# Four transformer blocks on one core: GpSimd takes the ends of 24 splits, SyncE takes the small transfers of the maxima, and the work is put in another order

## The reference

```python
    xn = _adaln(x, noise_emb, ln1_w, ln1_b)
    q, k, v = jnp.split(xn @ qkv_w.T, 3, axis=-1)
    q = _rope(q.reshape(B, L, N_HEADS, HEAD_DIM))
    k = _rope(k.reshape(B, L, N_HEADS, HEAD_DIM))
    sa = _attn(q, k, v) @ sa_out_w.T
    x = res + sa
    ...
    q = _rope((xn @ q_w.T).reshape(B, L, N_HEADS, HEAD_DIM))
    k = _rope((context @ k_w.T).reshape(B, L_ctx, N_HEADS, HEAD_DIM))
    v = (context @ v_w.T).reshape(B, L_ctx, N_HEADS, HEAD_DIM)
    x = res + _attn(q, k, v) @ ca_out_w.T
    ...
    h = jax.nn.gelu(xn @ ffn_w1.T + ffn_b1, approximate=False)
    x = res + (h @ ffn_w2.T + ffn_b2)
```

## Time and profile before

| | us |
|---|---|
| median of 3 runs | 2908.04 |
| lowest and highest | 2906.6, 2916.17 |
| the profiled execution | 2916.84 |
| its span | 2915.0 |

### The profile page before, as it was taken

The page is one execution under the profiler, slowest core; times in us unless marked ns, Lnnn a source line. Parts: engine busy times, 40 slices in busy tenths (PEclk is TensorE's granted clock), DMA queues, the critical chain, the costliest instruction groups (busy, mean ns, idle before and its releaser), DMA issues. The chain is left out here.

```text
span 2915.0 us, 47676 instructions
## 1 busy us (share of the span) xinstructions
PE 2728.5 (94%) x15136; PEld 1351.8 (46%) x15136; DVE 1893.7 (65%) x4209; ACT 1425.8 (49%) x2579; POOL 590.3 (20%) x999
## 2 busy tenths in 40 slices
PE   8999999999989999999988888898999999999899
PEld 5444344335544424334455566656645323224456
DVE  5977388642574783866344889668974884885621
ACT  3455635574445583566644444333221674785441
POOL 2110001131331110331125323411020010112510
PEclk9999999999999999999998999999999999999899
DMA  6333122433452312233066516521420322123621
GB/s 207 69 104 107 41 72 71 112 89 98 144 172 53 114 51 67 91 115 95 22 186 186 167 50 195 146 85 60 147 60 1 116 60 52 45 61 108 183 92 38
DMA packets 268153, 286.78 MB, mean 98 GB/s; under 512 B 70665, under 2 KB 207243, under 8 KB 267275
## 3 DMA queue, kind: packets, MB, share of 16 engines
q1 hardware_dynamic: 256651, 282.28, 33.0%
q0 software_dynamic: 11264, 1.46, 0.3%
HBM read 167.43 MB, written 114.72 MB: 97 GB/s over the span
## 5 line engine op out<-in xcount | busy, mean ns | idle before, releaser
L1570 ACT ACTIVATE probs<-ring_b 128x512 f32<-128x512 f32 (+1 forms) x1728 | 921.8, 599 | 457.9 <-PE ring_b L1429 359.9
L1748 DVE TENSOR_REDUCE row_max<-ring_a 128x1 f32<-128x1024 f32 x512 | 602.0, 1218 | 151.7 <-PE ring_a L1385 150.9
L1429 PE MATMUL ring_b<-q_ring,k_ring 100*128 100x512 bf16 x1536 | 526.8, 381 | 10.5 <-ACT probs L1570 2.8
L1385 PE MATMUL ring_a<-k_ring,q_ring 96*128 96x512 bf16 x1536 | 450.1, 383 | 27.9 <-DVE row_max L1748 16.1
L1462 PE MATMUL ring_c<-probs,v_and_ones 128*17 128x512 f32 x3072 | 402.0, 599 | 1.8 <-ACT probs L1570 1.2
L1745 DVE CUSTOM_DVE_ANT_0 w_mlp<-ring_a,w_mlp 128x1024 bf16<-128x1024 f32 x256 | 302.1, 1222 | 49.6 <-PE ring_a L1385 48.4
L1868 POOL CAST neg_max_parts<-neg_max 16x128 bf16<-16x128 f32 x112 | 37.6, 336 | 1392.1 <-ACT neg_max L1564 1141.3
L1429 PEld LDWEIGHTS ring_b<-q_ring,k_ring 100*128 100x128 bf16 x1536 | 145.7, 97 | 349.9 <-issue 241.5
L1385 PEld LDWEIGHTS ring_a<-k_ring,q_ring 96*128 96x128 bf16 x1536 | 135.5, 98 | 250.5 <-issue 153.6
L1485 PE MATMUL ring_b<-h_feat,w_mlp 128*128 128x512 f32 x512 | 230.3, 595 | 1.4 <-ACT h_feat L1541 0.8
L1497 PE MATMUL ring_a<-w_mlp 128*128 128x256 f32 x1024 | 226.1, 380 | 5.0 <-DVE w_mlp L1803 2.4
(11 more groups left out here) (143 smaller groups left out, 3346.4 us busy)
## 6 DMA issues: line engine op xcount, KB each, us to landing
q_ring<-scr_q SPq DMA_DIRECT2D x128, 384.0 KB, 4.3
scr_q<-split SPq DMA_DIRECT2D x64, 384.0 KB, 2.6
k_ring<-scr_k SPq DMA_DIRECT2D x64, 384.0 KB, 5.0
scr_q<-split SPq DMA_DIRECT2D x64, 256.0 KB, 3.0
scr_out<-out_stage SPq DMA_DIRECT2D x128, 128.0 KB, 2.5
scr_out<-out_stage SPq DMA_DIRECT2D x64, 256.0 KB, 2.4
h_feat<-scr_out SPq DMA_DIRECT2D x56, 256.0 KB
reciprocals<-scr_recip SPq DMA_DIRECT2D x56, 256.0 KB
```

What stands on the lines that cost most here:

```text
L1385: last = mm(ps[:, half * BLOCK:(half + 1) * BLOCK], q[0:PARTS, h, t * P:(t + 1) * P], k_view(g)[0:PARTS, h, half * BLOCK:(half + 1) * BLOC ...
L1429: last = mm(ps[:, :], k_view(g)[0:ROWS, h, s.kt * P:(s.kt + 1) * P], q[0:ROWS, h, q0:q0 + BLOCK], start=not g.masked, stop=True)
L1570: f(PT[0:n, s.pt, :], ps[0:n, :], ACT.Exp, **kw).then_inc(b_evac, 1)
L1748: v.tensor_reduce(NM[:, s.nm, s.u:s.u + 1], ps, AX.X, ALU.max).then_inc(a_evac, 1)
```

## The change

Three things change. The tails of layer 3's splits (without the context keys) become a step of their own on GpSimd, so a split of layer 3 is now `rotate` on TensorE and VectorE and then `tail` on GpSimd. `max_put` is issued by SyncE, not by GpSimd, with the same transfers. And the rank tables, REACH and DELAY have other numbers; with them the planner writes another order. The planner's own durations for the two steps change with them. The waits for a finished split ask which of the two kinds it is.

```diff
 RANK = dict(
...
-    load=(20, -1.2, 0.8, -3.2),
+    load=(-12, -9, -9, -9.2),
...
-    tk=(10.1, 0.1, -12, 9.9),
-    tk_s=(-0.5, 6.1, -9.2, -5.2),
+    tk=(13.2, 6.3, -9, -9),
+    tk_s=(6.8, 14.8, -5.3, 4.8),
...
-REACH = dict(PE=0.0, ACT=0.0, DVE=0.05, POOL=0.0, SP=0.2)
-DELAY = (7.5, 100)
+REACH = dict(PE=0.0, ACT=0.05, DVE=0.05, POOL=0.05, SP=0.0)
+DELAY = (7.5, 260)
...
+TAILS = (3,)
...
-        d = yield do("split", ([("PE", 0.264 if ck else 0.86)] if rope else []) + [("DVE", (2.08 if rope else 0.84) if ck else 4.3 if rope else 1.79)],
-                     after=[s], ring="a" if rope else None, counts=["split_n"], of=s, rope=rope, l=l)
+        if rope and l in TAILS and not ck:
+            t = yield do("rotate", [("PE", 0.86), ("DVE", 2.55)], after=[s], ring="a", counts=["turned_n"], of=s, l=l)
+            d = yield do("tail", [("POOL", 3.5)], after=[t], counts=["tail_n"], of=s, turned=t, l=l)
+        else:
+            d = yield do("split", ([("PE", 0.264 if ck else 0.86)] if rope else []) + [("DVE", (2.08 if rope else 0.84) if ck else 4.3 if rope else 1.79)],
+                         after=[s], ring="a" if rope else None, counts=["split_n"], of=s, rope=rope, l=l)
...
-        s = yield do("max_put", [("POOL", 2.15 if g.edge else 1.67)], after=[d], lat=2.6 if g.cross else 1.9, g=g, ms=ms, of=d)
+        s = yield do("max_put", [("SP", 1.4 if g.edge else 1.05)], after=[d], lat=2.2 if g.cross else 1.8, g=g, ms=ms, of=d)
...
+        def split_ended(eng, d):
+            if d.kind == "tail":
+                eng.wait_ge(tail_done, d.tail_n + 1)
+            else:
+                eng.wait_ge(split_done, d.split_n + 1)
...
+                elif s.kind == "max_put":
+                    g = s.g
+                    sp.wait_ge(max_split, s.of.msplit_n + 1)
+                    for j in range(3):
+                        sp.dma_start(QR[PARTS + 1 + j:PARTS + 2 + j, g.q, :], MS[:, s.ms, j, :]).then_inc(max_in[g.q], 16)
+                    if g.edge:
+                        sp.dma_start(QR[PARTS:PARTS + 1, g.q, :], KR[PARTS:PARTS + 1, 0, :]).then_inc(max_in[g.q], 16)
...
-                        link(v.tensor_copy(parts[:, 0, :], r))
+                        if s.kind == "rotate":
+                            v.tensor_copy(parts[:, 0, :], r).then_inc(turned, 1)
+                        else:
+                            link(v.tensor_copy(parts[:, 0, :], r))
...
+                elif s.kind == "tail":
+                    f = s.of
+                    r = RAW[:, f.raw, 0:f.width]
+                    parts = SPLIT[:, f.split, :, 0:f.width]
+                    pool.wait_ge(turned, s.turned.turned_n + 1)
+                    link(g_.tensor_tensor(out=r, in0=r, in1=parts[:, 0, :], op=ALU.subtract))
+                    link(g_.tensor_copy(parts[:, 1, :], r))
+                    g_.tensor_tensor(out=parts[:, 2, :], in0=r, in1=parts[:, 1, :], op=ALU.subtract).then_inc(tail_done, 1)
```

More of the change, by code:

```diff
@@ L1344, in _ @@
                     last.then_inc(b_full, 1)
-                elif s.kind == "split" and s.rope:
+                elif s.kind == "rotate" or s.kind == "split" and s.rope:
                     f = s.of
@@ L1680, in _ @@
                     parts = SPLIT[:, f.split, :, 0:f.width]
[L1681 removed]
+                    if s.kind == "rotate" or s.rope:
                         dve.wait_ge(tables_in, 16 * 3)
```

60 lines of the change are left out of this document (27 added, 33 removed).

## The result

| | before | after |
|---|---|---|
| median, us | 2911.37 | 2949.16 |
| lowest and highest | 2906.6, 2916.17 | 2945.16, 2950.99 |
| the profiled execution | 2916.84 | 2949.32 |
| its span | 2915.0 | 2947.5 |
| mean granted clock | 0.976 | 0.971 |

The ratio is 1.0128, with a 95% interval from 1.0105 to 1.0151: 38 us slower, where 12 faster was forecast. In after's listing the scores are L1436, L1441 and L1448 (L1417, L1422, L1429 before), the first products L1404 and L1414 (L1385, L1395), the fills L1308 and L1312 (L1289, L1293).

A forecast was written before the change was run, and what follows sets the result against it. TensorE's waiting, with VectorE bounding one stretch, was taken as what can shorten the kernel. Tails -10 and +4, SyncE 0 and order -6 gave -12 us on the median 2908: 2896 us, range 2866 to 2926.

The forecast's parts named there:

- What bounds the kernel: Whole kernel: only less TensorE waiting, bare or filled (about 430 us, 15%), shortens it; one stretch is bound by VectorE.
- Part 1, the tails: Layer 3: tails of 24 splits go to GpSimd; -10 us in VectorE's stretch (-14 to +2), +4 in cross queries.
- The lock between the engines: VectorE's stretch: instructions with two SBUF operands held while GpSimd runs; +2.4 us, bounds nothing to 12.8.
- The rival that I drew from it: VectorE's stretch: every tail meets a held VectorE instruction, making the term about 0 and not -10; no separate chance given.
- The cross queries: Layer 3's eight cross-query splits, 2645 to 2780 us: slower GpSimd tails on a path cost +4 us, between 0 and +9.
- Hidden, 0: Batch 1's eight self-attention tails, 2260 to 2310 us: worth 0, hidden by batch 0's self-attention.
- Part 2, the maxima on SyncE: Maxima and edge-row transfers go from GpSimd to SyncE: 0 us, between -7 and +33, over 15 TensorE waits.
- The slower rival: Window and cross attention: maxima queue on SyncE, late ones hold loads; +32 us before other terms, 2928 us, chance 0.19.
- Part 3, the order: Same work reordered: -4 us around VectorE's stretch, -2 from 18 fewer fills; -6 us, between -16 and +10.
- An unforeseen wait in a new place: Within the order's term, a bound: 5% of 186 us of bare TensorE idle, 10 us.
- signs of "right": VectorE without gaps, that part some 10 us shorter, GpSimd subtraction about 1.3 us, maxima waits near 30 us.
- signs of "wrong": VectorE waiting or stretched beyond 1 us, maxima waits above 50 us, lower clock in dense stretches, new idle in layers 0, 1.

The follow-up runs named there:

- o_put_sp: The kernel before, its order kept on every engine, but the maxima transfers are issued by SyncE instead of GpSimd: 2934.36 us, ratio 1.0078.

## Why the prediction was wrong, point by point

**What bounds the kernel** held in the main: VectorE's stretch answered to less work on VectorE, and in the dense stretches TensorE waits for single transfers. One row was read too widely. The 18.3 + 11.5 us of waits for the maxima are those of the whole span; in the two dense stretches they are 9.0 and 10.1 us.

**Part 1, the tails: right in kind, too small, and its cover misjudged.** For VectorE's stretch I had -10; at equal work it is -13.9 in after and -7.9 in the old order. The row of after over that work (columns as in the earlier trace rows) is shorter than the 118.1 us of before, with VectorE still the bound:

```profile
2036.00:2140.00 104.00, 90.99 (x604) 61.18 (x603) 101.75 (x508) 26.43 (x43) 30.73 (x29) 0.97 0.35 104
```

A tail is 3 and not 4 us on GpSimd (count: duration ns min/median/max):

```profile
L1880 POOL TENSOR_TENSOR raw<-raw,split x24: 1152/1158/1649, 2045.2 to 2762.7; 128x512 f32<-128x512 f32 x24
L1881 POOL CAST split<-raw x24: 611/611/952, 2046.8 to 2763.9; 128x512 bf16<-128x512 f32 x24
L1882 POOL TENSOR_TENSOR split<-raw,split x24: 1152/1157/1677, 2047.5 to 2764.6; 128x512 bf16<-128x512 f32 x24
```

I had scaled a cast by a pass with two operands, and it takes half. The lock between the engines is there: seven of 24 rotations' multiplications took over 1 us where one did before (three of the seven under a shift of the top-k scores, as that one, and four under a tail), and the four instructions of all 24 rotations together grew from 60.6 to 68.4 us. That is 7.8 us in the kernel, of which I had 2.4 for the 6 tails in the stretch. The Trainium skill (SBUF — State Buffer, "Who interferes with whom") has the lock as a rule, and the trace agrees. The rival that I drew from it, that every tail would meet such an instruction and the term be 0, did not come: seven of 24 rotations had this multiplication held, and the runs show a gain. The cross queries were to lose 4 us by the slower tail; they won 1.2 (old order) and 6.4 us (new), and why is not shown: VectorE is busy only 79 of 135 us there. "Hidden, 0" for batch 1 was 4.9 us in the new order. Part of what the tails bring in the new order is only what that order loses without them.

**Part 2, the maxima on SyncE: the step that failed is its value, 0 for what is +12 to +21.** My range had the true size (-7 to +33), and I took the middle row. I had priced the transfer itself, issue plus landing. That was the part without a surprise (the maxima's line in o_put_sp with its issue in ns, min/median/max, and its landing, then the landing in after):

```profile
L1228 SPq DMA_DIRECT2D q_ring<-neg_max_parts x336: 502/589/1586, 94.5 to 2807.2; - x168
...
DMA to landing us min/median/max: 1.6/2.1/7.3
```

```profile
DMA to landing us min/median/max: 1.6/1.8/6.6
```

3 x 0.59 + 2.0 = 3.8 us, where GpSimd needs 3.5. The Trainium skill (DMA: Bandwidth & Descriptors, the table at its head) gives SyncE's path the earlier first byte; the medians here, 1.8 to 2.1 against 2.0, show neither clearly ahead. What cost lies outside that price, in the queue. In the old order SyncE begins 32 of 112 groups more than 1 us after they are cut (16 by GpSimd), and the issue of the last of the three rows ends 2.81 us after the cut in the mean, where GpSimd has 2.22. And each group takes some 1.8 us of SyncE from the loads behind it. GpSimd itself, which cuts the maxima, also waits longer for the rows of earlier groups to land: 15.3 us in o_put_sp and 18.2 in after, where it was 4.4. The slower rival named both ("Maxima that come late now hold those loads") and its size, +32 before the other terms, was nearer than my value; but the sign I gave for it, waits for the maxima above 50 us, did not show: 34.1 in after. It was sought at the wrong place, since in the places shown the delay landed on the transfer behind. In layer 3's cross-attention, the place that part 2 had named, the waits for query loads went from 2.0 us in before to 6.2 by the order and to 9.2 with SyncE.

**Part 3, the order: the step that failed most, -6 for +25.5.** I took 4 us from eight first reductions that stand earlier and 2 us from 18 fewer fills elsewhere. Fills are sized by the waits that the planner expects, so fewer fills say only that the planner expects less. The chip waited 25.4 us more, and with nothing in it. "An unforeseen wait in a new place" had 10 us in my bounds; two such places took 18.5 and 12.5. I had read the order only around VectorE's stretch, where the planner counts well (planned -14.8, trace -13.9), and not at the two places where it shows its own loss of 5 to 6 us. I had also taken the three parts as independent, and they are not: the order costs 51 us with neither move and 25.5 with both.

**The sum.** -12 was -10 + 4 + 0 - 6. Made in this sequence, the runs say -6.5 (tails), +18.2 (SyncE, 11.7 + 6.5) and +25.5 (order), together +37.2 on the median of before, against 37.8. The sum is right by construction, and another sequence splits it otherwise: order first it is +51.0 (order), -27.5 (tails) and +11.9 (SyncE). In both the order is the largest loss, SyncE a smaller one and the tails a gain. Had the order been worth nothing, the result would have been 2924, inside the range.

**What would show it.** VectorE without gaps and a shorter part, GpSimd's subtraction of 1.16 us, waits for the maxima near 30: these signs of "right" all came. Of the signs of "wrong" three came: casts and rotations beyond 1 us (up to 1.53), new idle time in layer 0, of which I had written that I foresaw none, and a lower clock in dense stretches, 0.66 where before has 0.97 at 820 to 840 us.

**What stays open.** Of the order's 25.5 us, 13.7 went with layer 0's numbers, and why is only argued (VectorE's late row maxima). For the other 12 the traces show the place (work 1500 to 1550, which before ends at 1883 us, with weights and gate behind waiting transfers), but moving one of them up only swapped waits, and fewer bytes changed little. A third order, from a planner with longer landing times, ends level with the old one; it changes so much else that it does not say what the loss was. That single landings spread widely around their median (L1219: median 5.0, up to 10.0 us) and the planner uses one figure fits all of this, but was not tested by itself. How SyncE's 18 us divide between late loads, late maxima and the clock is open too.

## What to carry to other kernels

Price a transfer that changes its queue by what stands behind it there, not by its own issue and landing: here the landing was equal and the move cost 12 to 21 us, by the order and the place of the tails. Before trusting a new order of a planner, look for the places where it plans a small loss itself: here two such losses of 5 to 6 us came back two and three times as large. To judge a change that comes with a new order, keep the order and move only the steps: it split 38 us into -6.5, +18 and +25.5 with three runs. Then go the other way too, from the new order back. Here that gave +51, -27.5 and +12, so the parts depend on each other, and a single split must not be taken for their worth.

## What the runs showed of the hardware

A cast of 128x512 from fp32 to bf16 on GpSimd takes 0.61 us where the subtraction of two operands takes 1.16. A single issue on SyncE can take long among others: the context values' load, with 0.95 us in the median, took 4.93 us once, at 1881.48 us (4.36 us at most in before), and nothing else was issued meanwhile. A VectorE multiplication with two SBUF operands, 0.68 us in the median, took 1.17 to 1.41 us in seven of 24 rotations, each time while an instruction of GpSimd with SBUF operands ran that had begun before it. And raising the mean granted clock from 0.971 to 0.988 took some 41 us off the needed multiplications but only 13 us off the kernel.
